# A decoder of two layers on one core: retrieval parts taken in pairs, a softmax mask moved to TensorE, and identity products at stage ends

## The reference, cut to what matters

```python
x = x + L0_attn(norm(x))              # linear attention with a decay scan
x = x + L0_xattn(norm(x), ids, ctx)   # 4 experts, chosen by token number
x = x + L0_ffn(norm(x))               # retrieval, below
x = x + L1_attn(norm(x))              # convolution, attention in blocks of 16 tokens, 8 heads
x = x + L1_xattn(norm(x), ctx)        # cross attention with rounded numbers
x = x + L1_ffn(norm(x))               # 16 routed experts and a shared one
```

```python
sim = einsum('pbthn,hkpn->pbthk', q, keys);  scores, idx = top_k(sim, 8)
all_scores = sx[..., :, None] + sy[..., None, :];  sc, pk = top_k(all_scores, 8)
z = act(einsum('btd,bthkd->bthk', h, down_embed[indices]) * softmax(sc))
out = einsum('bthk,bthkd->btd', z, up_embed[indices])
```

## Time and profile before

| | us |
|---|---|
| runs | 1102.94, 1104.35, 1115.01 (median 1104.35) |
| profiled execution | 1114.29 |
| its span, first to last instruction | 1112.5 |
| busy: PE, DVE, POOL, ACT | 816.8, 787.1, 545.7, 498.8 |
| mean granted clock of TensorE | 0.806 of full speed |

### The profile page before, as it was taken

The page is one execution under the profiler, slowest core; times in us unless marked ns, Lnnn a source line. Parts: engine busy times, 40 slices in busy tenths (PEclk is TensorE's granted clock), DMA queues, the critical chain, the costliest instruction groups (busy, mean ns, idle before and its releaser), DMA issues. The chain is left out here.

```text
span 1112.5 us, 13294 instructions
## 1 busy us (share of the span) xinstructions
PE 816.8 (73%) x4554; PEld 535.1 (48%) x4577; DVE 787.1 (71%) x1309; ACT 498.8 (45%) x715; POOL 545.7 (49%) x394
## 2 busy tenths in 40 slices
PE   5987989767777785776779957666666767567990
PEld 2553654345655664655663346552333333435550
DVE  4756266399999999999851357669999998233552
ACT  2312113345546546545430132369888887113530
POOL 2207000489779798797730012218777776150005
PEclk9978989968887887888889557897777787568995
DMA  4011030000000000000016000088999999013113
GB/s 156 1 35 42 1 120 1 0 1 1 1 0 1 1 1 1 1 1 0 1 38 230 0 1 1 15 281 154 188 166 176 171 182 165 16 66 123 39 70 120
DMA packets 152544, 71.31 MB, mean 64 GB/s; under 512 B 138779, under 2 KB 148445, under 8 KB 151326
## 3 DMA queue, kind: packets, MB, share of 16 engines
q1 hardware_dynamic: 150942, 66.27, 26.2%
q0 software_dynamic: 1536, 4.20, 1.2%
HBM read 27.46 MB, written 9.44 MB: 33 GB/s over the span
## 5 line engine op out<-in xcount | busy, mean ns | idle before, releaser
L726 POOL TENSOR_TENSOR r_pairs<-r_side_exp 128x1035 f32<-128x1035 f32 x128 | 248.3, 1969 | 8.9 <-DVE r_w L891 7.8
L809 ACT ACTIVATE r_w<-r_w,r_scale 128x1001 f32<-128x1001 f32 (+1 forms) x128 | 144.4, 1139 | 162.8 <-DVE r_w L891 141.1
L781 PE MATMUL r_head_sum<-ident,r_w 128*128 128x128 f32 (+1 forms) x1024 | 154.6, 316 | 85.3 <-ACT r_w L809 62.5
L781 PEld LDWEIGHTS r_head_sum<-ident,r_w 128*128 128x128 f32 (+1 forms) x1024 | 141.3, 168 | 106.7 <-ACT r_w L809 80.1
L1596 ACT ACTIVATE c_probs<-c_scores,c_bias,c_q_scale 128x1024 int16<-128x1024 f32 x128 | 154.2, 1204 | 30.9 <-DVE c_bias L1609 22.1
L1607 DVE TENSOR_REDUCE c_neg_max<-c_scores 128x1 f32<-128x1024 f32 x128 | 155.5, 1215 | 7.0 <-PE c_scores L1547 6.8
L1534 POOL CAST kv_parts<-c_probs 128x1024 bf16<-128x1024 int16 x128 | 132.4, 1041 | 55.2 <-ACT c_probs L1596 54.3
L883 DVE SCALAR_TENSOR_TENSOR r_chosen<-r_pairs,r_kept,r_z 128x1024 f32<-128x1024 f32 (+1 forms) x112 | 141.3, 1275 | 13.1 <-ACT r_sims L793 4.3
L1547 PE MATMUL c_scores<-c_kT,c_placed 128*128 128x512 bf16 x233 | 96.6, 499 | 60.0 <-ACT c_probs L1596 55.9
L891 DVE TENSOR_TENSOR r_w<-r_pairs,r_chosen 128x1024 f32<-128x1024 f32 (+1 forms) x112 | 134.7, 1204 | 0.0
L757 PE MATMUL r_head_sum<-r_up,r_wT 128*128 128x256 f32 (+1 forms) x256 | 73.6, 458 | 13.5 <-ACT r_wT L820 13.5
(11 more groups left out here) (287 smaller groups left out, 1468.2 us busy)
## 6 DMA issues: line engine op xcount, KB each, us to landing
sorted_rows<-b_zeros SPq DMA_DIRECT2D x1, 3072.0 KB, 20.4
e_row<-sorted_rows SPq DMA_DIRECT2D x6, 512.0 KB, 6.3
expert_rows<-e_made SPq DMA_DIRECT2D x6, 512.0 KB, 2.9
en_w<-in_w SPq DMA_DIRECT2D x1, 2992.0 KB, 12.6
ew_w<-in_w SPq DMA_DIRECT2D x1, 2992.0 KB, 12.1
ew_w_near<-in_w_near SPq DMA_DIRECT2D x1, 2176.0 KB, 19.4
r_up<-in_up SPq DMA_DIRECT2D x1, 2048.0 KB, 10.4
c_pT<-kv_parts SPq DMA_TRANSPOSE x128, 3.3
```

The lines of the kernel that those rows point to most:

```text
L726: nc.gpsimd.tensor_tensor(pairs[:, v % MADE, :].rearrange("p (a b) -> p a b", b=KEYS), a.broadcast_to([P, ROWS, KEYS]), b.broadcast_to([P, ...
L781: last = nc.tensor.matmul(head_sum[0:m, b // 4, (b % 4) * P:(b % 4 + 1) * P], w[:, v % RING, b * P:b * P + m], ident[:, :], start=(h == 0 ...
L809: nc.scalar.activation(w[:, v % RING, 0:COLS[f]], w[:, v % RING, 0:COLS[f]], ACT.Silu, scale=scale[:, t % 2, h:h + 1]).then_inc(silu_done, 1)
```

## The change

```diff
+def keep_busy(nc, bank, ident, count):
+
+    for n in range(count):
+        nc.tensor.matmul(bank, ident[:, :], ident[:, :].rearrange("p (o n) -> p o n", o=1).broadcast_to([P, HALF // P, P]),
+                         start=True, stop=True)
```

2. Retrieval:

```diff
-        MADE, RING = 8, 14
+        MADE, RING = 10, 14
-        BY_POOL, LEAD = (2, 5), 4
-        BELOW_AT, EXP_AT, SUM_AT, ADD_AT, PROJECT_AT = 7, 3, 0, 5, 5
+        BY_POOL, LEAD = (0, 1), 4
+        BELOW_AT, EXP_AT, SUM_AT, ADD_AT, PROJECT_AT = 0, 0, (0, 0), (0, 5), (2, 3)
-        wT = sb("wT", [P, PB, P])
+        wT = sh.ctxT[:, :, :].rearrange("p c n -> p (c n)")[:, 0:PB * P].rearrange("p (b n) -> p b n", n=P)
+            def best_grid(t):
+                pool.wait_ge(exps_ready, t + 1)
+                if t >= 1:
+                    pool.wait_ge(kept_ready, t)
+                ...
+                nc.gpsimd.tensor_tensor(grid..., a, b, ALU.mult).then_inc(grid_ready, 1)
-                if h == PROJECT_AT and k + 1 < HALVES:
+                if h == PROJECT_AT[f] and k + 1 < HALVES:
-            for v in range(PARTS_R):
+            for v in range(0, PARTS_R, 2):
                 k, t, f, h = place(v)
                 if h == 0 and f == 0:
                     best_pairs(t)
-                if h == 0 and f == 1 and t + 1 < NT:
-                    best_keys(t + 1)
+                    if t + 1 < NT:
+                        best_keys(t + 1)
                 pick(v)
-                if v >= 1 and not by_pool(v - 1):
-                    weigh(v - 1)
-                if f == 0 and h == ADD_AT and t >= 1:
+                pick(v + 1)
+                for n in (v, v + 1):
+                    if not by_pool(n):
+                        weigh(n)
+                if (f, h + 1) == ADD_AT and t >= 1:
                     residual(t - 1)
-            weigh(PARTS_R - 1)
```

3. Blocks: the mask and a copy of the identity are bf16; PE first writes the mask to each scores bank with one product of 512 columns and adds the scores on top of it; DVE takes only the maxima, negated, from PSUM; ACT takes eight exponentials of 128 columns with the negated maximum as bias; `p` has three buffers; `join(t - 1)` stands ahead of `score(t + 2)`; DVE adds the join's bias before the next maxima:

```diff
+                for j in range(2):
+                    nc.tensor.matmul(scores[:, t % 2, j, :], s.identb[:, :], s.mask[...]...,
+                                     start=True, stop=False, skip_group_check=True)
-                nc.scalar.activation(p[:, t % 2, :, :], p[:, t % 2, :, :], ACT.Exp).then_inc(exp_done, 1)
+                for n in range(HEADS_B):
+                    last = nc.scalar.activation(p[:, t % PROBS, n, :], scores[...], ACT.Exp, bias=neg_max[:, t % 2, n:n + 1])
-                nc.vector.tensor_tensor(p[...], scores[...], s.mask[...], ALU.add).then_inc(masked, 1)
-                chain.step(nc.vector.tensor_reduce(row_max[:, t % 2, :], p[:, t % 2, :, :], AX.X, ALU.max))
-                nc.vector.tensor_tensor(p[...], p[...], row_max[...], ALU.subtract).then_inc(shifted, 1)
+                nc.vector.tensor_reduce(neg_max[:, t % 2, :], scores[...], AX.X, ALU.max, negate=True).then_inc(max_ready, 1)
```

More of the change, by code:

```diff
@@ L452, in _ @@
             norm_tensor(nc, pe, ln, ident)
+            keep_busy(nc, out[:, 1, :], ident, 7)
             pe.wait_ge(loaded, 32)
@@ L834, in _ @@
                 silu(v)
-                if h == SUM_AT and k >= 1:
+                if h == SUM_AT[f] and k >= 1:
                     copy_sums(k - 1)
@@ L938, in block_attention @@
         s.proj = sb("proj", [WIDTH + 1, D])
-        s.mask = sb("mask", [P, P])
+        s.mask, s.identb = sb("mask", [P, P], BF16), sb("identb", [P, P], BF16)
+        s.mask_ready = sem("mask_ready")
         s.loaded = sem("out_loaded")
@@ L1094, in score @@
                 if t >= 2:
-                    pe.wait_ge(masked, t - 1)
+                    pe.wait_ge(exp_done, t - 1)
+                for j in range(2):
+                    nc.tensor.matmul(scores[:, t % 2, j, :], s.identb[:, :],
+                                     s.mask[:, :].rearrange("p (o n) -> p o n", o=1).broadcast_to([P, CB, P]),
+                                     start=True, stop=False, skip_group_check=True)
                 for h in range(HEADS_B):
@@ L1109, in turn @@
                 for n in range(HEADS_B):
-                    last = nc.tensor.transpose(turned[:, n // CB, (n % CB) * P:(n % CB + 1) * P], p[:, t % 2, n, :], ident[:, :])
+                    last = nc.tensor.transpose(turned[:, n // CB, (n % CB) * P:(n % CB + 1) * P], p[:, t % PROBS, n, :], ident[:, :])
                 last.then_inc(turned_ready, 1)
@@ L1153, in exps @@
             def exps(t):
-                act.wait_ge(shifted, t + 1)
-                nc.scalar.activation(p[:, t % 2, :, :], p[:, t % 2, :, :], ACT.Exp).then_inc(exp_done, 1)
+                act.wait_ge(max_ready, t + 1)
+                if t >= PROBS:
+                    act.wait_ge(turned_ready, t - PROBS + 1)
+                for n in range(HEADS_B):
+                    last = nc.scalar.activation(p[:, t % PROBS, n, :], scores[:, t % 2, n // CB, (n % CB) * P:(n % CB + 1) * P],
+                                                ACT.Exp, bias=neg_max[:, t % 2, n:n + 1])
+                last.then_inc(exp_done, 1)
             exps(0)
@@ L1200, in _ @@
             dve.wait_ge(s.loaded, 48)
-            prepare(0)
-            prepare(1)
+            maxima(0)
+            maxima(1)
             sums(0)
@@ L1206, in _ @@
                     sums(t + 1)
+                if t >= 1:
+                    residual_a(t - 1)
                 if t + 2 < NT:
-                    prepare(t + 2)
+                    maxima(t + 2)
                 if t >= 1:
-                    residual(t - 1)
-            residual(NT - 1)
+                    residual_b(t - 1)
+            residual_a(NT - 1)
+            residual_b(NT - 1)
 HEADS_C = 16
```

66 lines of the change are left out of this document (36 added, 30 removed).

## The result

| | us |
|---|---|
| kernel after, four runs | 1046.9 to 1049.41, median 1048.12 |
| kernel before, four runs | 1102.94 to 1115.01, median 1103.89 |
| ratio after to before | 0.9473, 95% interval 0.942 to 0.9527 |
| profiled execution after, its span | 1046.9, 1044.2 |
| busy: PE, DVE, POOL, ACT | 798.3, 743.4, 547.2, 502.9 |

The kernel is 55.8 us faster by the medians; 48.6 were forecast, and 1048 lies in the range (1036 to 1082), 8 us under the predicted 1056.

The account below looks back on a forecast made before the run. DVE was taken to pace the retrieval, POOL near behind, and a cycle of waits the block attention. Savings 29.8 + 10.3 + 3.8 + 1.5 + 3.2 = 48.6 us off the median 1104.35 gave 1056; range 1036 to 1082.

Parts of the forecast that it names:

- (a): Retrieval: the grid moves from DVE to POOL, saving 17.4 us over seven tiles and adding 0.96 to POOL's tile.
- (b): Retrieval: pairs of picks and weighings avoid a 0.19 us stall seven times a tile, 10.6 us for eight tiles.
- (e): Retrieval: projections placed earlier; the residual's 1.22 us wait stays about as it is, no gain and no loss.
- (c): Retrieval: `best_keys(1)` moves from between halves into DVE's wait ahead of the first pick, 1.8 us gained once.
- (d): Retrieval: POOL weighs heads 0 and 1; no cost while POOL's 38.2 us stays below DVE's tile of 40.3.
- the front: Block attention up to the first sums: one set of maxima, eight exponentials and the mask's products, gain 3.0 us.
- the cycle: Block attention, from one tile's transposes to the next: 7.44 us becomes 6.4, 7.3 us over seven tiles.
- Identity products: PE products at stage ends to raise its clock: 3.8 us for `token_experts`, 1.5 for `weigh_experts`, net 3.2 for `attend`.
- 1 (POOL the bound): Retrieval: POOL becomes the bound with a tile of 42.7 us, total 1074 us; chance 0.17.
- 2 (waiting projections): Retrieval: waiting projections keep PE at half clock, making the kernel slower, 1118 us; chance 0.04.
- 3 (blocks and identity products give nothing): Block attention and stage ends: no gain there, only the retrieval's 29.8 us counts, 1075 us; chance 0.10.
- 4: Whole kernel: nothing moves, within 1%, as pairs bring new waits about the size of the old; chance 0.03.

Follow-up runs that it names:

- e10: Kernel before with only DVE's picks and weighings put in pairs, grid still on DVE and heads 2 and 5 for POOL: 1086.72 us, ratio 0.987.
- e8: Kernel after with the pairs taken out, back to DVE's old order of picks and weighings: 1083.51 us, ratio 0.9814.
- e11: Kernel after with the projections late, at head 5 of both halves as before, in place of heads 2 and 3: 1054.72 us.
- e2: Kernel before with only the seven calls for identity products added: 1096.41 us, ratio 0.9965.
- e6: Kernel after without all seven calls for identity products: 1051.4 us.
- e3: Kernel before with only the retrieval's changes, no identity products: 1066.37 us, ratio 0.9647.
- e4: Kernel before with only the block attention's changes, including the mask's tile: 1086.21 us, ratio 0.9822.

## Why the prediction was right, and where it wasn't

**Retrieval: 33.2 to 29.8.** (a) The grid came off DVE as said, and cost POOL 1.11 us (L723, 1102 to 1135 ns), where 0.96 was taken; POOL's tile of 38.2 is 37.5, in part since one of its two weighings took 1.96 us where both had taken 2.3. (b) The stall of 0.19 us and the count of seven fit e10: its waits for `z` and the residual are 4.2 us in place of 10.7, its grid takes 2.33 us in place of 2.47, and of its 16.8 us some 9 to 10 are left when these are taken off. The 10.6 were right as a term. Missed was that the waits shrink: 4.6 us in the kernel after in place of 10.7, most of it the residual's, which (e) left as it was and only the upper bound of 38 took in. That is more than the 3.4 by which the stage came out better. The terms were added as if each stood alone. They don't: e8 shows that (a), (c), (d) and (e) without (b) are worth 0, mostly because the maxima that (c) moves away were the cover of `z`. The tile came to 39.1 us where 40.3 were worked out and 40 were named as the sign.

(e) Wrong. "I count no gain and no loss" for the earlier projections; e11 has 7.7 us. Both sides were seen, `z` at half clock against an earlier start, but the start was not given its price: over the stage late projections make DVE wait 7.7 us more for `z` (9.4 against 1.7) and 2.2 more for the residual (5.1 against 2.9).

**Blocks: 15.6 to 10.3.** Against the short execution the front gave 3.3 (8.57 to 5.27; 3.0 taken) and the cycle 12.4 (7.29 to 5.52; 7.3 taken). The rows that the prediction had are of the long execution, where both were slower. The cycle is 5.52 us, not 6.4: the step that failed is "PE's own work was 39.0 us for some seven tiles, 5.6 a tile at clock 0.84", with 6.0 to 6.5 worked out from it for the mask. The clock was held fixed. Between the first and the last transposes of the kernel after it is 0.96, and PE's work, mask included, 35.5 us for seven tiles, 5.1 each. PE is busy there for 92% of the time, so that little of the cycle is left to waits. Of the values given, the lower bound of 5.4 was the nearest. The exponentials took 2.18 us for eight, as estimated.

**Identity products.** In all 8.5 were taken; the medians have 4.9 (e2) or 3.3 (e6). First stages 4.0 (3.8 taken). The convolution's own gain is 3.5 (1.5 taken), and the half clock of some executions wasn't known at all: the earlier trace rows end before it, and no row over the 64-row products was read. That is also the error in "against the median": the 9.9 us between the profiled execution and the median were one stretch, whose length the change alters. `quantise`: nothing was expected, it loses 1.8. `attend` and `route`: net 3.2 was taken, it is 0.9 where the clock rises and a loss where not; the delay of 3.0 lay in its bounds (0.3 to 3.7), the gain of 3.1 on the logits was no sure one.

**The rule against it.** The prediction set the rows of the rising clock against the Trainium skill (TensorE: Matmul & The Clock Gate, Part 4: PE-mode transpose). The kernel after shows the same, with products that the code issues as `is_transpose=True`: from 219.20 to 222.80 us PE does nothing but L799's transposes after a pause of 5.67, at 0.54, and from 222.80 to 225.80 it has 0.98, with nothing but transposes in between. The windows:

```profile
219.20:222.80 3.60, 2.99 (x14) 3.00 (x15) 3.60 (x4) 1.69 (x2) 3.60 (x3) 0.54 0.00 0
222.80:225.80 3.00, 0.47 (x4) 0.23 (x2) 3.00 (x4) 2.28 (x2) 3.00 (x3) 0.98 0.00 0
```

**The rivals.** 1 (POOL the bound): POOL waits for DVE once a tile (14.2 us in all), and DVE, once the picks have begun, for nothing of POOL's; POOL has 1.6 us left in a tile, though, so it would be the next bound. 2 (waiting projections): its mechanism is real and is what e8 shows, half clock over `z` and waits of 2.19 us; with the pairs it isn't reached. 3 (blocks and identity products give nothing): no for the blocks; for the products at `attend` nearly so. 4: no. Of the signs named, the clock was 1.00 at the start of the three stages (L459, L601 and L1005 of before, from 90, 156 and 548 us in the kernel after), and 0.99 from the transposes of `route` on to the logits.

**The right answer's reasons.** That the two large terms stand, each by itself, is shown by e3 and e4. That DVE paces the retrieval is shown by its 38.74 us of work in a tile of 39.10; of the blocks only the cycle's new length is shown, not which part of the change made it. That the total was only 7 us off is in part luck, since errors of different signs met: the blocks 5.3, retrieval 3.4 and convolution 2.1 better, the last stages 4.1 worse.

## What to carry to other kernels

Look for what covers a wait before moving it: an independent pass of 1.8 us moved out from between two halves cost some 14 us of waits against the 19 by which DVE's work was shorter (e8), until pairs of instructions gave new cover. When a median and a profiled execution differ by a per cent, take a second trace and compare the stages before anything is added to either. Identity products at the end of a stage paid here where PE was at full clock (the first stages, the convolution); where it was at half clock they ran at nearly double their length and brought the clock back in three traces of five, and where the next stage waited for a DMA the clock fell again in five traces of six.

## What the runs showed of the hardware

- TensorE's granted clock can go to half in the midst of dense work: over products with 64 rows it was 0.52 for 32 us with PE busy 31.81, after pauses of only 0.84 and 0.19 us, which an execution at 1.00 has as well. Three traces show it, and by their times 15 of 59 executions of one and the same program are of this kind.
- The same four products at half clock brought the clock back for the following stage in three traces and not in two.
- On POOL the product of two broadcast operands, 512 columns, takes 1.11 us, less than half of DVE's median of 2.47 in the kernel before. The same DVE instruction took 2.33 in e10, and 0.69 at its fastest, ahead of the first pick; no run here shows why.
- Two independent DVE operations of 1,024 columns follow each other after 1.13 to 1.20 us though each is shown as 1.2 to 1.3 long; one that waits for its forerunner starts 0.1 us after its end. At seven such places in a tile that is 10.6 us, 3% of the retrieval.
